# Two transformer layers on one core: weight copies ahead in the expert rounds, first-layer experts and first-half routing earlier

## The reference

```python
xn = layernorm(x)
x = x + causal_attention(xn @ wq.T, xn @ wk.T, xn @ wv.T)  # rotary, 4 x 1024 tokens
      + moe_top1(xn)       # 8 experts of 128x128, 512 places each, gate = softmax prob
xn = layernorm(x)
u, v = xn @ Wu + bu, xn @ Wv + bv
h = filter_mlp(positions) * exp(-0.01 t)                   # two gelu layers
x = x + (u * irfft(rfft(v, 2048) * rfft(h, 2048))) @ Wo + bo
      + moe_top2(xn)       # 8 experts, relu(xs @ W1 + b1) @ W2 + b2, weighted by the probs
```

## Time and profile before

| | us |
|---|---|
| median of 3 runs | 483.1 |
| lowest, highest | 481.83, 484.2 |
| the profiled execution: its time | 485.89 |
| the profiled execution: its span | 484.1 |
| TensorE busy | 371.5 (77%) |
| VectorE busy | 288.8 (60%) |
| ScalarE busy | 224.9 (46%) |
| GpSimd busy | 239.0 (49%) |

### The profile page before, as it was taken

How to read it: one execution, slowest core, us unless ns; L and a number is a source line. 1 busy time by engine, 2 the same in 40 slices (tenths; PEclk the granted TensorE clock), 3 DMA queues, 4 the chain that set the end, 5 groups by cost and what they waited for, 6 DMA issues and landing times.

```text
span 484.1 us, 7795 instructions
## 1 busy us (share of the span) xinstructions
PE 371.5 (77%) x2300; PEld 301.1 (62%) x2300; DVE 288.8 (60%) x786; ACT 224.9 (46%) x551; POOL 239.0 (49%) x246
## 2 busy tenths in 40 slices
PE   0796789899998887969988779999878879555520
PEld 0662255687784566637977669899767768554520
DVE  4956655927753894483798946597557853332105
ACT  1453243344342236532430156556647777666604
POOL 2502676505665132036566666666666664545440
PEclk9998989999998997997998979999989999999985
DMA  9999999057311510001011563444422226324007
GB/s 208 278 263 312 171 172 154 29 137 250 87 57 45 142 44 1 1 22 39 23 34 44 145 190 92 129 143 147 125 62 78 61 60 213 91 64 141 31 11 254
DMA packets 64744, 55.05 MB, mean 114 GB/s; under 512 B 6819, under 2 KB 56683, under 8 KB 64446
## 3 DMA queue, kind: packets, MB, share of 16 engines
q1 hardware_dynamic: 57888, 41.71, 35.3%
q0 software_dynamic: 6656, 12.51, 8.5%
q10 hardware_dynamic: 158, 0.33, 0.4%
HBM read 30.44 MB, written 25.27 MB: 115 GB/s over the span
## 4 chain that ended last, share of the span: by engine, by line
PE 32%; issue 22%; DVE 13%; ACT 11%; POOL 9%; DMA 7%; SPq 2%; ACTq 2%; POOLq 1%; DVEq 0%
PE psS L1148 16%; PE psO L1148 10%; POOL slots L839 5%; POOL moe L849 5%; ACT ring L1038 4%; PE psT L1148 3%; DMA slots<-row,slot 2%; ACT hT L1110 2%; SPq L701 2%; ACT row L1010 1%; ACTq L1037 1%; DVE work L1730 1%; DMA work<-in_wvg 1%; DMA moe<-ys,xs 1%; DVE xres L1764 1%
## 5 line engine op out<-in xcount | busy, mean ns | idle before, releaser
L826 POOL DMA_INDIRECT slots<-row,slot x64 | 67.0, 1046 | 56.6 <-issue 28.5
L849 POOL DMA_INDIRECT moe<-ys,xs x61 | 63.2, 1036 | 55.7 <-issue 27.3
L1038 ACT ACTIVATE ring<-w 128x642 f32 x80 | 55.8, 759 | 3.3 <-issue 3.3
L839 POOL DMA_INDIRECT slots<-row,slot x32 | 33.8, 1056 | 38.4 <-DVE slot L1559 20.5
L849 POOL DMA_INDIRECT moe<-ys,w x35 | 37.4, 1069 | 27.7 <-DVE ys L1894 14.0
L1003 ACT ACTIVATE work<-psT 128x512 f32<-128x512 f32 (+3 forms) x32 | 16.5, 516 | 64.4 <-PE psT L1264 52.4
L1148 PE MATMUL psS<-work 128*128 128x512 f32 (+3 forms) x96 | 40.6, 535 | 4.7 <-DVE work L1723 2.9
L993 ACT ACTIVATE work<-psS,work 128x128 f32<-128x128 f32 (+7 forms) x32 | 23.7, 740 | 37.8 <-DVE work L1734 37.3
L1148 PE MATMUL psO<-work 128*128 128x128 f32 x288 | 38.1, 279 | 0.0
L1148 PE MATMUL psO<-xsT,ring 128*128 128x128 f32 x160 | 23.1, 289 | 19.1 <-ACT ring L1038 18.9
L1148 PE MATMUL psT<-xsT,ring 128*128 128x128 f32 x160 | 22.1, 281 | 19.6 <-ACT ring L1038 19.2
(11 more groups left out here) (285 smaller groups left out, 847.9 us busy)
## 6 DMA issues: line engine op xcount, KB each, us to landing
slots<-xs SPq DMA_DIRECT2D x14, 516.0 KB, 12.7
mats<-in_iv SPq DMA_DIRECT2D x16, 256.0 KB
xs<-slots SPq DMA_DIRECT2D x61, 64.5 KB
w<-in_w SPq DMA_DIRECT2D x8, 321.0 KB
w<-slots SPq DMA_DIRECT2D x35, 64.5 KB
xres<-in_x SPq DMA_DIRECT2D x4, 512.0 KB, 9.6
moe<-xs SPq DMA_DIRECT2D x4, 512.0 KB, 9.4
mats<-in_fw SPq DMA_DIRECT2D x1, 2048.0 KB, 10.0
```

The lines of the kernel that those rows point to most:

```text
L826: pool.indirect_dma_start(slots1[:, :], bass.IndirectOffsetOnAxis(ap=(slot1, slot2)[k][:, i:i + 1], axis=0), row[:, i, :], None, bounds_ch ...
L839: pool.indirect_dma_start(dst[:, :], bass.IndirectOffsetOnAxis(ap=slots[:, i:i + 1], axis=0), row[:, i, :], None, bounds_check=bound, oob_ ...
L849: pool.indirect_dma_start(dst[:, :], bass.IndirectOffsetOnAxis(ap=row_slots[l][m][:, D:ROWW].bitcast(I32), axis=0), ys[:, n % UNROLL, :], ...
L1038: act.activation(pair_w[p % RING_PAIRS][:, t, :], w12[:, bass.ds(e, 1), :].rearrange("p e h -> p (e h)"), ACT.Copy).then_inc(e_w, 1)
```

## The change

Five edits:

1. ScalarE's rounds: `copy_weights(r+2)` and `take_rows(r+2)` now stand ahead of `hidden(r+1)`.
2. First-layer experts: `expert0_out` stands ahead of the transposes of its row, `expert0_bias` directly behind the row's maximum. The filter's spectra move from rows 9 and 10 to rows 17 and 18; the radix step stays in rows 6 to 8.
3. Token numbers are replaced by eight tiles, each before the eight dispatches that need them, where before sixteen were replaced at once.
4. Additions, norms, gates, counts and routing of the first half move up by one row; for the gates only the first two, for the norms only the first four entries.
5. The two `inverse_std` in the scatter stand before the issues 6 and 14, where they stood before 4 and 12.

```diff
-FILT_RADIX_AT, FILT_DFT_AT = 6, 9
+FILT_RADIX_AT, FILT_RADIX_ROWS, FILT_DFT_AT = 6, 3, 17
-GATES_AT = (24, 25, 29)
-NORM_AT = {23: [(0, 0), (0, 1)], 24: [(1, 0), (1, 1)], 27: [(2, 0)], 28: [(2, 1)]}
-COUNTS_AT = 27
+GATES_AT = (23, 24, 29)
+NORM_AT = {22: [(0, 0), (0, 1)], 23: [(1, 0), (1, 1)], 27: [(2, 0)], 28: [(2, 1)]}
+COUNTS_AT = 26
-ADD_BEFORE_MAX = {22: (4, 8), 23: (12, 16), 25: (20, 24), 29: (24, 28), 31: (28, 30)}
-ADD_BEHIND_ROW = {21: (0, 4), 22: (8, 12), 24: (16, 20)}
+ADD_BEFORE_MAX = {21: (4, 8), 22: (12, 16), 25: (20, 24), 29: (24, 28), 31: (28, 30)}
+ADD_BEHIND_ROW = {20: (0, 4), 21: (8, 12), 23: (16, 20)}
...
-NORM_IN_SCATTER = (4, 12)
+NORM_IN_SCATTER = (6, 14)
...
             for g in range(2):
                 second_ids(0, g)
-            pool.wait_ge(ids_done, 4)
-            for i in range(HT):
-                dispatch(0, 1, i)
+                pool.wait_ge(ids_done, 3 + g)
+                for i in range(HT // 2 * g, HT // 2 * (g + 1)):
+                    dispatch(0, 1, i)
...
             for r in range(PRELUDE, PAIRS1):
+                if 0 <= r + 2 < PAIRS1:
+                    copy_weights(r + 2)
+                    take_rows(r + 2)
                 if 0 <= r + 1 < PAIRS1:
                     hidden(r + 1)
-                if 0 <= r + 2 < PAIRS1:
-                    take_rows(r + 2)
-                    copy_weights(r + 2)
...
                     scores(n + 1)
+                for e in expert0_at(n - 1):
+                    expert0_out(e)
                 if n in FILT_AT:
...
                     expert0_rows(e)
-                for e in expert0_at(n - 1):
-                    expert0_out(e)
...
                     row_max(n + 1)
+                for e in expert0_at(n - 1):
+                    dve.wait_ge(moe0_w_loaded, 32)
+                    expert0_bias(e)
                 dve.wait_ge(exp_done, n + 1)
```

More of the change, by code:

```diff
@@ L165 @@
 FILT_AT = (0, 2)
-FILT_RADIX_AT, FILT_DFT_AT = 6, 9
+FILT_RADIX_AT, FILT_RADIX_ROWS, FILT_DFT_AT = 6, 3, 17
 SPLIT_AT = 12
-GATES_AT = (24, 25, 29)
-NORM_AT = {23: [(0, 0), (0, 1)], 24: [(1, 0), (1, 1)], 27: [(2, 0)], 28: [(2, 1)]}
-COUNTS_AT = 27
+GATES_AT = (23, 24, 29)
+NORM_AT = {22: [(0, 0), (0, 1)], 23: [(1, 0), (1, 1)], 27: [(2, 0)], 28: [(2, 1)]}
+COUNTS_AT = 26
 WARM_COUNTS, WARM_FILTER, WARM_GATES, WARM_SCORES, WARM_COUNTS_2 = 7, 7, 7, {24: 3}, 6
-WARM_PROBS = {5: 4, 7: 3, 9: 3, 19: 7, 23: 6, 27: 3, 29: 14}
+WARM_PROBS = {5: 4, 7: 3, 9: 3, 19: 7, 22: 6, 26: 3, 28: 14}
 PARTS = (slice(0, 96), slice(32, 64), slice(64, 96), slice(64, 96))
@@ L177 @@
 GROUP = CAP // P
-ADD_BEFORE_MAX = {22: (4, 8), 23: (12, 16), 25: (20, 24), 29: (24, 28), 31: (28, 30)}
-ADD_BEHIND_ROW = {21: (0, 4), 22: (8, 12), 24: (16, 20)}
-ROUTING_BEFORE_MAX = {26: 6, 28: 8}
-ROUTING_BEHIND_ROW = {26: 6, 27: 10, 28: R1_STEPS}
+ADD_BEFORE_MAX = {21: (4, 8), 22: (12, 16), 25: (20, 24), 29: (24, 28), 31: (28, 30)}
+ADD_BEHIND_ROW = {20: (0, 4), 21: (8, 12), 23: (16, 20)}
+ROUTING_BEFORE_MAX = {25: 6, 27: 8}
+ROUTING_BEHIND_ROW = {25: 6, 26: 10, 27: R1_STEPS}
 W_RING = 6
@@ L539, in two_layer_kernel @@
                 T_USES += [("f", 2 * (n - FILT_DFT_AT) + u) for u in range(2)]
+            O_USES += [("y", e) for e in expert0_at(n - 1)]
             if n:
@@ L542, in two_layer_kernel @@
             T_USES += [("x", e) for e in expert0_at(n)]
-            O_USES += [("y", e) for e in expert0_at(n - 1)]
             if gates_at(n):
@@ L895, in dispatch_second @@
                 k, i = second_half[j]
-                if k and i == 0:
-                    for g in range(2):
-                        second_ids(1, g)
-                    pool.wait_ge(ids_done, 6)
+                if k and i % (HT // 2) == 0:
+                    second_ids(1, 2 * i // HT)
+                    pool.wait_ge(ids_done, 5 + 2 * i // HT)
                 dispatch(1, k, i)
@@ L1807, in _ @@
                     attention_row(n - 1)
-                if FILT_RADIX_AT <= n < FILT_DFT_AT:
-                    for _ in range(RAD_F // (FILT_DFT_AT - FILT_RADIX_AT) + 1):
+                if FILT_RADIX_AT <= n < FILT_RADIX_AT + FILT_RADIX_ROWS:
+                    for _ in range(RAD_F // FILT_RADIX_ROWS + 1):
                         next(filter_radix, None)
@@ L1814, in _ @@
                     tt(bias[PARTS[k], :], bias[PARTS[k], :], biasb[PARTS[k], :], ALU.subtract).then_inc(split_sub, 1)
-                for e in expert0_at(n - 1):
-                    dve.wait_ge(moe0_w_loaded, 32)
-                    expert0_bias(e)
                 if n in ADD_BEHIND_ROW:
```

## The result

The changed kernel takes 466.94 us (median; 466.87 to 468.51) against 483.25 us for the kernel before: a ratio of 0.967, 95% interval 0.964 to 0.970. The forecast was 463 us, range 457 to 472. The profiled execution took 466.87 us with a span of 465.0 us, against 485.9 and 484.1 before. So from profile to profile 19 us are gone, from median to median 16.3.

The account below looks back on a forecast made before the run. ScalarE's closed ring of 3.98 us a round was taken to hold GpSimd up, with attention's end also setting the finish. Gains 15.5 + 0.95 + 3.0 + 0 + 0.5 = 20 us, taken from the 483.1 median: 463 us, range 457 to 472.

Parts of the forecast that it names:

- ScalarE's closed ring: Late rounds: hidden matmuls, activations, take and weight copies follow one another in a loop of 3.98 us a round.
- a sign of being wrong: Rounds: a period between 3.3 and 4 us with GpSimd still waiting for VectorE would show the forecast wrong.
- Part 1: ScalarE's rounds, weights first: GpSimd becomes the bound; gain 15.5 us, bounds 10 and 17 plus 2.
- The loss through the convolution rounds: Six rounds with transposes and projections: TensorE needs 3.78 us each, costing 4.6 us without stock; 1.5 us taken as lost.
- three loops: Loops left in the rounds: ScalarE's work 2.68 us, weight-slot ring taken as 2.7, TensorE 3.78 in six rounds, else under 3.
- Part 3: First-half scatter: 14 transfers instead of 12 before the stop for statistics; everything behind moves up 3.0 us.
- Part 2: First rounds: pair 0's weights copied before its rows arrive; first result about 5 us sooner, 0.95 us gained.
- Rival C: Rounds keep 3.98 us because TensorE waits for the take or activations; only 4.5 us gained, 479 us; chance 0.04.
- Part 4: Token numbers by eight tiles: one more copy and wait on GpSimd in each half; 0 us, bounds -0.5 and +1.
- Part 5: Attention rows: moved spectra, experts and additions end attention 0.5 us sooner, bounds -3 and +4; the least certain term.
- rival B: Attention ends 4 us later: TensorE idles in row 9, additions hold up two row maxima; 467 us; chance 0.08.
- Rival A: GpSimd's sends get longer as they crowd beside VectorE; 8 us lost, 471 us; chance 0.13.

Follow-up runs that it names:

- norm_alone: Kernel before, with only the last attention row's statistics asked for before the 7th and 15th first-half sends; ratio 0.9995 to the kernel before.
- order_undone: Changed kernel with ScalarE's old order in the rounds (activations, take, then weight copies); ratio 1.0025 to the kernel before.
- norm_undone: Changed kernel with the last row's statistics asked for before the 5th and 13th first-half sends, as before; ratio 0.9725 to the kernel before.
- order_alone: Kernel before, with only ScalarE's new order in the rounds (weight copy and take ahead of activations); ratio 0.9669 to the kernel before.
- three_apart: Changed kernel with GpSimd waiting after every third send instead of every second, with descriptor room 6144; ratio 0.9934 to the kernel before.

## Why the prediction was right, and where it was not

**The mechanism held.** ScalarE's closed ring was the bound, its order was the largest part by far, and GpSimd set the pace of the last 15 rounds, not of 28: from 403.87 to 447.66 us its pairs start 43.8 / 14 = 3.13 us apart, with 1.5 us of waits above a full queue. The 15 pairs before them, from 352.74, are 51.1 / 15 = 3.41 us apart, in the range (3.3 to 4 us) that I had named as a sign of being wrong; of their 5.8 us above a full queue some 2 are waits and the rest longer sends. The order was priced at 15.5 + 0.95 = 16.45 us; alone it gives 233.6 - 216.9 = 16.7.

**Part 1.** Taken 15.5 us. Alone, 16.4 in the rounds; in the changed kernel 176.3 - 162.7 = 13.7. The loss through the convolution rounds was taken as 1.5 us. The last 60 sends have 35.7 us of idle time where a full queue has 32.1: 3.6 us. (The sends themselves are 1.3 us shorter than before, and the stage in front of them, 286.29 to 352.74, is 1.1 us longer.) From 359.46 to 408.15 the results come 48.7 / 13 = 3.75 us apart, slower than GpSimd sends.

The forecast listed three loops, ScalarE, the ring and TensorE, and left out VectorE. Before, VectorE was busy 16.72 of 20.79 us at the start of these rounds, which is 3.2 us for a round of 3.98, already more than GpSimd's 3.02. In the changed kernel it is busy 26.24 of the 28.44 us from 355.02 to 383.46, its results come (380.77 - 355.02) / 7 = 3.68 us apart, and TensorE waits for VectorE's `work` twice (timeline of VectorE, then a row of the waits of TensorE: us in total, times, longest):

```profile
355.02 0.42 DVE L1892 TENSOR_TENSOR ys<-psS,ring 128x256 f32<-128x256 f32 x1
...
380.77 0.42 DVE L1892 TENSOR_TENSOR ys<-psO,ring 128x256 f32<-128x256 f32 x1
381.11 2.35 DVE L1855 TENSOR_TENSOR work<-work 128x1024 f32<-128x1024 f32 x2
```
```profile
PE psS L1404 <- DVE work L1855: 4.0, 2, 2.1
```

TensorE is nearly as full, 38 of the 44 us from 353 to 397, and no run separates the two. After two results 5.7 us behind the one before, at 386 and at 396 us, the stock is gone. The first stands behind TensorE's second wait for `work` (2.05 us, at 383.51) and eight matmuls that took 1.92 us instead of 1.06; what held the second the profile does not name. Timelines of VectorE, ScalarE, TensorE in the changed kernel:

```profile
390.21 0.42 DVE L1892 TENSOR_TENSOR ys<-psO,ring 128x256 f32<-128x256 f32 x1 [0.30 <-PE psO L1147]
...
395.95 0.42 DVE L1892 TENSOR_TENSOR ys<-psS,ring 128x256 f32<-128x256 f32 x1 [0.89 <-remote]
```
```profile
397.09 1.38 ACT L1037 ACTIVATE ring<-w 128x642 f32 x2 [2.44 <-DVE ys L1892]
```
```profile
398.79 1.16 PE L1147 MATMUL psT<-xsT,ring 128*128 128x128 f32 x8 [1.61 <-ACT xsT L1102]
```

GpSimd's waits of 1.93 and 1.21 us at 397 and 400 us, shown above, follow from it. In its last 60 sends 3.7 us are put to `ys`.

**Parts 2 and 3.** Taken 0.95 + 3.0; from the statistics to the first return the changed kernel is 57.2 - 52.2 = 5.0 us shorter. The step that was missing is that they are not two terms. Without the order Part 3 is worth nothing (norm_alone, order_undone), because the first result then comes no sooner. With it Part 3 brings some 3 us at the end (2.3 to 3.3 by norm_undone against the changed kernel's two executions): 4.4 to 4.7 up front, of which the rounds take some back. I said that "everything behind them moves up by 3.0 us"; that was true only because Part 2 had moved the first result, by 6 us and not 5 (49.8 us behind the last `mv` in order_alone instead of 55.9). Rival C, which kept 4.5 us for the other parts under the old period, would have come out near 483, not 479.

**Part 4.** Taken 0; 0 in time.

**Part 5.** Taken 0.5 us; the last statistics came 0.4 sooner, but both moves undone give the same time. Its inner numbers were worse than its sum. Row 20 was to be 1 us late on TensorE and was 4.2 (project(3, 0) at 156.70 against 152.52), since the spectra cost 2 x 3.74 us and the waits behind them did not shrink as much. The first send of the first layer came at 108.40, not 105.5, because TensorE, idle where the spectra had stood, came back at the lower level of its clock: granted 0.50 (1.2 of 2.4 GHz) from 101 to 104 us, where before it had 1.00 (that stretch, the kernel before first, in the columns of the earlier trace rows; then the TensorE timeline of the changed kernel, beside the earlier trace rows):

```profile
101.00:104.00 3.00, 2.72 (x18) 1.78 (x17) 1.10 (x3) 1.61 (x3) 0.00 (x0) 1.00 0.61 140
```
```profile
101.00:104.00 3.00, 2.76 (x6) 1.31 (x7) 0.00 (x0) 0.60 (x1) 0.00 (x0) 0.50 0.60 147
```
```profile
101.11 1.94 PE L1297 MATMUL psT<-cst,xs 128*128 128x128 f32 x4 [4.62 <-DMA xs<-slots]
...
170.94 1.50 PE L1147 MATMUL psS<-xT,work 128*128 128x512 f32 x2 [2.27 <-ACT work L992]
```

The last row is a stall in attention row 22, put to ScalarE's exponential; the maximum that this needs now stands behind VectorE's additions, as rival B had it. The first half's sends start only 0.5 us sooner (211.13). On another chip, one execution of each, the two moves even cost 0.8 us at the last `mv`; so the -0.5 was right partly by luck, and it lay in slack, since GpSimd's stop took it in.

**Rival A.** The sends did not get longer: 33.7 + 28.6 = 62.3 us for 60, against 63.6. (The 0.2 us "on average" of the forecast held for one stretch; over the 60 it was 5.4 / 60 = 0.09.) Beside a VectorE that is busy 17.96 of 19.56 us they took 13.65 / 12 = 1.14 us each, and 33.20 / 34 = 0.98 in the last stretch:

```profile
352.74:372.30 19.56, 17.22 (x147) 16.33 (x146) 17.96 (x32) 15.45 (x40) 13.65 (x12) 1.00 0.22 64
...
397.20:449.91 52.71, 33.91 (x267) 30.88 (x267) 15.87 (x49) 38.89 (x103) 33.20 (x34) 0.95 0.38 114
```

The Trainium skill (SBUF — State Buffer, section "SBUF: two separate sides") says that VectorE and GpSimd share a port pair as an exclusive lock, and it names the VectorE instructions that take it: those in a two-port mode, or with two inputs in SBUF beside a GpSimd operation that reads SBUF. The rows do not show which instructions took it; if all of the lengthening is its doing, it costs 0.17 us a send in the densest stretch, 4 us in all, far less than a whole VectorE instruction for each send.

**The sum.** From profile to profile 20 us were forecast and 19 measured. Part 1 gave 1.8 us less than taken and Parts 2 and 3 gave 1.0 more; that they nearly cancel is luck. The last step failed by more: I took the same 20 us from the median, though the profiled execution of before lay 2.8 us above it. Profile and median of the changed kernel agree (466.87 and 466.94), so the median moved 16.3 us. On a second chip it was 485.68 - 468.45 = 17.2. That is 3 of the 4 us between 463 and 467; the fourth is Part 1's loss less what the start gave.

## What to carry to other kernels

Where a loop over pairs of tiles closes through one engine, ask which of that engine's steps another engine needs first, and put the steps that prepare a later pair (weights and rows, both of them) ahead of those that finish the present one. Work taken off an engine that feeds such a loop is worth nothing until the loop itself starts sooner: check each term of a sum for whether it stands without the others. When a loop gets shorter, list the work of every engine in one turn of it, also of one that is far from full over the whole kernel (VectorE, 60% here, had 3.2 us in each turn). And take a difference of profiles from a profile, not from a median that lies elsewhere.

## What the runs showed of the hardware

- GpSimd's gap behind a second send, 0.77 us, takes in small work: with two fills of 0.14 us in it the pair grew by 0.07 us.
- Waiting after every third send instead of every second one, with room for the descriptors of three, changed the pattern of gaps from 0.30, 0.77 to 0.30, 0.30, 0.77 (0.89 in a part of the scatter, with either pattern) and sent faster (61.0 against 64.0 us for the same 40 transfers), but the kernel as a whole was slower.
- A dispatch is not always 0.97 us: in norm_alone one took 6.36 us and one 2.87.
- TensorE, after gaps, was granted 0.66 of its full clock over 10 us in three_apart, where the changed kernel, without gaps, had 1.00 in these 10 us. Four 128x128 transposes took 1.94 us behind a wait of 4.62 us, at a granted clock of 0.50, and 0.60 without a wait.
